# The key compares of the count table: four slots in one fp16 tensor-tensor compare, read by PE with a step

## The chip, the cores and the metric

The kernel runs on one core of one Trainium2 chip. The metric is the device time of one execution in microseconds. The kernel before took 5724.34 us, the median of three runs (5718.58 to 5726.55). Engines are called by their names in the profile: PE (TensorE, with PEld for its weight loads), DVE (VectorE), ACT (ScalarE), POOL (GpSimd), SP (SyncE, which here only issues DMAs; SPq is its queue).

## The reference, cut to what matters

Four graph layers run one after the other on 6250 nodes of 128 features and 100000 edges `(src, dst)`, sorted by `dst`. The first of them is, three times:

```python
msgs = h[src] * (src != dst)
agg = segment_sum(msgs, dst, num_segments=N)
x_neigh = agg @ W_conv[l] + b_conv[l]
h = relu(concatenate([x_neigh, h]) @ W_upd[l] + b_upd[l])
```

The sum over edges is linear in `h`, so it is a product with a table of counts: how many edges go from node `src` to node `dst`. The kernel builds this table once and uses it in three layers here and again in the last graph layer. Only the building of the table is touched by the change.

## The kernel before, in words

**The table.** It is the DRAM tensor `A_d`, 128 partitions (the low seven bits of `src`) by strips of `KEYS` = 392 fp16 numbers (49 blocks of `src` times 8 neighbouring `dst`). It is built in `BSLOTS` = 1184 slots. A slot takes 256 edges as two halves (`h` or `k` 0 and 1) of 128 edges, one edge per partition. For each half DVE writes two one-hot matrices: `src_hot`, which of 128 source rows the edge has, and `key_hot`, which of the 392 keys it has. PE multiplies them, 128 weight columns (`src_hot`) by 392 moving columns (`key_hot`), and adds into a PSUM bank.

**The DVE part** (lines 915 to 931). A group is `HOTS` = 4 slots, so there are 296 groups. At the head of a group, one tensor-tensor compare (line 924) writes the `src_hot` of all four slots and both halves: 128 rows by 8 = 1024 fp16 elements, in which the 8 values of a row lie side by side. It compares `count_up` (each number repeated eight times) with `vals` (the eight values of the group, repeated over the rows). Then each slot has two tensor-scalar compares (line 928), one for each half, of the contiguous row of 392 keys with one number per partition. `key_hot` has a buffer for each of four slots; the slot's buffers are free when PE has counted the slot four earlier (line 926). `hots_ready` goes up by one for each slot.

**The PE part** (lines 1588 to 1600). For each slot PE waits until ACT has emptied far enough (`evacuated`, line 1593), clears a bank with a matmul of one column and zero weights (line 1594), waits for `src_ready` and `hots_ready`, and issues the two matmuls of line 1598, which raise `counted`. The weights are read from `src_hot` with a step of 8 elements (16 bytes); the moving matrix `key_hot` is contiguous. Every four slots PE loads eight bank numbers into registers (line 429, called at 1591).

**The ACT and SP part.** ACT copies one bank per slot from PSUM into one of eight fp16 strips in SBUF (lines 1287 to 1294), once `counted` has it and the DMA that last read this strip has landed (`strip_out`). SP writes the strip to `A_d` with one DMA per slot (line 501), 98 KB, and loads eight row numbers into registers every eight slots (line 429, called at 499). The order on each queue is the program's order; no queue has other work in this stage. POOL waits for a DMA of this stage and does nothing in it.

**After the stage**, SP waits until all strips are in DRAM (lines 502 to 507) and loads the first blocks of the table (line 516); DVE removes the self loops from them (line 941) and PE multiplies (line 1634), which is the layer loop.

**Buffers.** `rg` holds `key_hot` and the two buffers of `src_hot`; `count_up` and `src_val` lie in plane 1 of `planes`, which is read again as table blocks after the stage.

Of the kernel before, what the change touches and what calls it, by code (L numbers as in the profile page):

```python
# [28 lines left out]
P = 128  # L29
# [31 lines left out]
KEYS = BLOCKS * STRIP  # L61
# [5 lines left out]
BSLOTS = -(-(ES_TILES + STRIPS + 1) // BODY) * BODY  # L67
BJ = -(-BSLOTS // P)
BPAD = BJ * P
BK = -(-ES_TILES // P)  # L70
BANKS = 8
# [3 lines left out]
HOTS = 4  # L75
# [57 lines left out]
def gnn(nc, io, out):  # L133
    fp32, i32, bf16, fp16 = mybir.dt.float32, mybir.dt.int32, mybir.dt.bfloat16, mybir.dt.float16
    DVE = mybir.EngineType.DVE
    ALU, ACT = mybir.AluOpType, mybir.ActivationFunctionType

    ctx = ExitStack()
    with ctx:
# [22 lines left out]
        pl = sb("planes", [P, 6, NP_])  # L162
# [3 lines left out]
        rg = sb("rg", [P, 2624])  # L166
# [42 lines left out]
        flat = ps[:, :, :].rearrange("p b n -> p (b n)")  # L209
# [22 lines left out]
        hots_ready, counted, evacuated = sem("hots_ready"), sem("counted"), sem("evacuated")  # L232
        src_ready = sem("src_ready")
# [117 lines left out]
        colT = pl[:, 0, 0:4 * BPAD].rearrange("p (w h s) -> p w h s", w=2, h=2)  # L351
        steps = pl[0:1, 5, 0:4 * BPAD].bitcast(i32)
        oh = onehot[:, :, :, :].rearrange("p a g n -> p (a g n)")
        key_row = oh[:, 0:KEYS // 2].bitcast(fp16)
# [5 lines left out]
        plan_i = oh[:, 624:624 + 4 * BJ].bitcast(i32).rearrange("p (j c) -> p j c", c=4)  # L360
        tiles_f = oh[:, 672:672 + 3 * BK].rearrange("p (n k) -> p n k", k=BK)
        tiles_i = oh[:, 688:688 + 2 * BK].bitcast(i32).rearrange("p (n k) -> p n k", k=BK)
        key_hot = rg[:, 0:HOTS * KEYS].bitcast(fp16).rearrange("p (b h n) -> p b h n", b=HOTS, h=2)
        src_hot = rg[:, HOTS * KEYS:HOTS * (KEYS + 2 * P)].bitcast(fp16).rearrange("p (b n t) -> p b n t", b=2, t=2 * HOTS)
        count_up = pl[:, 1, 2600:2600 + HOTS * P].bitcast(fp16).rearrange("p (n t) -> p n t", t=2 * HOTS)
        src_val = pl[:, 1, 3200:3200 + BPAD].bitcast(fp16).rearrange("p (h s) -> p h s", h=2)
        strips = scaled[:, :, :].rearrange("p a n -> p (a n)")[:, 0:BODY * KEYS // 2].bitcast(fp16).rearrange("p (b n) -> p b n", b=BODY)


# [76 lines left out]
        def _(sp):  # L446
# [49 lines left out]
            for s in range(BSLOTS):  # L496
                b = s % BODY
# [5 lines left out]
                sp.wait_ge(strip_out[b], 16 * (BSLOTS // BODY + 1))  # L503
            sp.wait_ge(st_plan, 64)

            sp.wait_ge(hots_ready, BSLOTS)
            sp.wait_ge(src_ready, BSLOTS // HOTS)
            for n in range(LAYERS * VB):
                u = n % VB
                k = VB_COLS[u] // STRIP  # L510
# [35 lines left out]
            for q in range(PAIRS):  # L546
# [7 lines left out]
                for u in (2 * q, 2 * q + 1):  # L554
                    k = VB_COLS[u] // STRIP
# [93 lines left out]
        def _(dve):  # L649
# [89 lines left out]
            for k in range(SJ):  # L739
                last = dve.tensor_scalar(cmp[:, k, :], iota_s, small[:, 2, k:k + 1], None, ALU.is_ge)  # L740
# [68 lines left out]
            def step(ins):  # L809

                planned_so_far[0] += 1
                ins.then_inc(planned, 1)
                dve.wait_ge(planned, planned_so_far[0])
# [12 lines left out]
            for k in range(BK):  # L826
                last = dve.tensor_scalar(later[:, k, 0:lead], at_slot, tiles_f[:, 1, k:k + 1], None, ALU.is_gt)
# [85 lines left out]
                    dve.tensor_tensor(q_rows[0][:, cut, 2, :], by_block(hb_rest[:, (c - 1) % 2, :]), q_rows[0][:, cut, 1, :], ALU.subtract).then_inc(q_low, 1)  # L913

            for h in range(2):
                last = dve.tensor_copy(src_val[:, h, :], colT[:, 1, h, :])
            step(last)
            step(dve.tensor_copy(count_up, key_row[:, 0:P].rearrange("p (n o) -> p n o", o=1).broadcast_to([P, P, 2 * HOTS])))
            for s in range(BSLOTS):
                if s % HOTS == 0:  # L920

                    dve.wait_ge(counted, BANKS + max(s - HOTS, 0))
                    vals = src_val[:, :, s:s + HOTS].rearrange("p (o h) s -> p o h s", o=1).broadcast_to([P, P, 2, HOTS])
                    dve.tensor_tensor(src_hot[:, s // HOTS % 2].rearrange("p n (h s) -> p n h s", h=2), count_up.rearrange("p n (h s) -> p n h s", h=2),
                                      vals, ALU.is_equal).then_inc(src_ready, 1)
                dve.wait_ge(counted, BANKS + s + 1 - HOTS)
                for h in range(2):
                    last = dve.tensor_scalar(key_hot[:, s % HOTS, h, :], key_row, colT[:, 0, h, s:s + 1], None, ALU.is_equal)  # L928
                last.then_inc(hots_ready, 1)

            dve.wait_ge(counted, BANKS + BSLOTS)

# [36 lines left out]
            for l in range(LAYERS):  # L969
                for u in range(VB + 2):  # L970
                    n, w = l * VB + u, VB_COLS[min(u, VB - 1)]
# [98 lines left out]
            for c in range(CHUNKS + LAG_O):  # L1070
# [5 lines left out]
                k = c - LAG_O  # L1076
# [15 lines left out]
            for c in NORM_V:  # L1092
                for b in range(c * CB, (c + 1) * CB):
                    last = dve.tensor_scalar(rows_view(3)[:, b, :], rows_view(1)[:, b, :], stat[:, 4, b:b + 1], stat[:, 1, b:b + 1], ALU.mult, ALU.add)
# [104 lines left out]
            for q in range(PAIRS + 1):  # L1199
                for k in range(TWOS if q < PAIRS else AT_SPLIT[1] + 1):  # L1200
                    if q < PAIRS:
# [8 lines left out]
                        n = IN_TWO[k]  # L1210
# [255 lines left out]
        def _(pe):  # L1466
# [121 lines left out]
            for s in range(BSLOTS):  # L1588
                b = s % (BODY // 2)
                if b == 0:  # L1590
                    banks = steps_at(mybir.EngineType.PE, 2 * s, BODY, (BANKS - 1) * 512)

                pe.wait_ge(evacuated, s + BANKS - 5)
                pe.matmul(flat[:, bass.ds(banks[2 * b], 1)], no_weights, key_row[:, 0:1], start=True, stop=True, skip_group_check=True)  # L1594
                pe.wait_ge(src_ready, s // HOTS + 1)
                pe.wait_ge(hots_ready, s + 1)
                for k in range(2):
                    last = pe.matmul(flat[:, bass.ds(banks[2 * b + 1], KEYS)], src_hot[:, s // HOTS % 2, :, k * HOTS + s % HOTS], key_hot[:, s % HOTS, k, :],  # L1598
                                     start=False, stop=True, skip_group_check=True)
                last.then_inc(counted, 1)  # L1600

# [321 lines left out]
```

## Time and profile before

| what | value |
|---|---|
| median of three runs | 5724.34 us |
| the profiled execution, from its first to its last instruction (span) | 5771.7 us |
| PE busy / DVE busy / ACT busy, share of the span | 86% / 63% / 47% |
| the stage of the count table, first to last strip DMA issued | 109.6 to 866.7 us |
| DVE / PE / ACT busy in 400 to 600 us, in the midst of it | 97% / 81% / 73% |

The profile gives for the profiled execution its span alone; no time around the span is shown for it. "Busy" is the time in which an engine ran an instruction that counts; the issue of a DMA does not count, so SP has no busy share. A group row reads: line, engine, operation, output<-input, count | busy us, mean ns of one | idle us before, and what ended that idle time. Durations of instructions that follow each other closely overlap in their pipelines, so the start-to-start time can be shorter than the duration.

### The profile page before, as it was taken

To read this page: it belongs to the slowest core of one execution; us is meant where nothing else is said; L and a number is where in the kernel's file an instruction comes from. 1 tells how busy PE (TensorE), PEld (TensorE's weight loads), DVE (VectorE), ACT (ScalarE), POOL (GpSimd) and SP (SyncE) were. 2 spreads that over 40 slices of the span, in tenths; PEclk is the share of its full clock that TensorE was granted. 3 is DMA by queue.
4 is the path that set the end of the run, shared out by engine and by line. 5 is a ranking of instruction groups with operands and counts; after the bars stand their busy time and mean duration, and the time that the engine had idled before them with its cause. 6 is when DMAs were issued, how large, how long until landed. Compare 5 with 4: busy or idle time off the path is not lost.

```text
span 5771.7 us, 104492 instructions
## 1 busy us (share of the span) xinstructions
PE 4992.4 (86%) x27719; PEld 3586.0 (62%) x27720; DVE 3660.0 (63%) x9507; ACT 2739.6 (47%) x7037; POOL 1847.7 (32%) x1948
## 2 busy tenths in 40 slices
PE   5888879999999997888888888688888888899998
PEld 3444447888888885444444444566666566677775
DVE  7999994443433444666666667555555555588886
ACT  4777771111111114766677667322222222488884
POOL 0000001100000002666666665566666666111111
PEclk9999999999999998888889888799999999999999
DMA  4554556555555552111112111233333333233330
GB/s 97 161 159 157 160 160 220 197 188 179 191 185 199 194 187 72 45 45 45 45 45 46 44 45 43 79 88 86 86 88 86 87 87 86 78 115 137 137 125 28
DMA packets 388581, 650.09 MB, mean 113 GB/s; under 512 B 91140, under 2 KB 329694, under 8 KB 363179
## 3 DMA queue, kind: packets, MB, share of 16 engines
q1 hardware_dynamic: 330844, 526.22, 27.4%
q0 software_dynamic: 57424, 120.01, 8.4%
q8 instruction: 157, 2.57, 0.2%
q14 instruction: 156, 1.28, 0.1%
HBM read 511.57 MB, written 134.42 MB: 112 GB/s over the span
## 4 chain that ended last, share of the span: by engine, by line
PE 55%; another core or an unknown queue 13%; DVE 9%; issue 9%; ACT 6%; SPq 3%; DMA 3%; DVEq 2%; POOL 1%; ACTq 0%; POOLq 0%
PE ps L1634 21%; PE ps L1691 14%; PE ps L1829 8%; SPq L501 3%; PE ps L1598 2%; DMA A_d<-scaled 2%; PE ps L1690 2%; PE ps L1519 2%; ACT ps L1401 1%; ACT scaled L1294 1%; DVE rg L928 1%; ACT planes L1406 1%; DVE planes L1047 1%; DVE onehot L795 1%
## 5 line engine op out<-in xcount | busy, mean ns | idle before, releaser
L575 POOL DMA_INDIRECT rg<-tab_L,idxT x832 | 811.8, 976 | 1499.5 <-DMA tab_L<-planes 1025.9
L1634 PE MATMUL ps<-planes 128*128 128x384 bf16 (+1 forms) x7350 | 1224.6, 327 | 20.0 <-DVE planes L941 16.6
L1634 PEld LDWEIGHTS ps<-planes 128*128 128x128 f16 (+1 forms) x7350 | 1036.8, 142 | 172.2 <-issue 22.3
L1354 ACT ACTIVATE scaled<-onehot,rg 128x128 f32<-128x128 f32 x2912 | 893.2, 388 | 397.9 <-PE ps L1691 230.8
L1691 PE MATMUL ps<-scaled,rg 128*128 128x512 f32 x1664 | 1032.2, 714 | 0.0
L1690 PEld LDWEIGHTS ps<-rg,onehot 128*128 128x128 f32 x1664 | 342.7, 215 | 747.9 <-issue 401.7
L1294 ACT ACTIVATE scaled<-ps 128x392 f16 x1184 | 547.9, 499 | 209.9 <-DMA A_d<-scaled 133.4
L805 DVE TENSOR_TENSOR planes<-planes,ps 128x128 f32 x832 | 239.5, 288 | 570.0 <-remote 473.2
L928 DVE TENSOR_SCALAR rg<-onehot,planes 128x392 f16<-128x392 f16 x2368 | 580.1, 320 | 16.5 <-PE ps L1598 11.7
L1598 PE MATMUL ps<-rg 128*128 128x392 f16 x2368 | 562.6, 362 | 25.4 <-DVE rg L928 5.0
L1047 DVE TENSOR_TENSOR planes<-planes,ps 128x512 f32 x832 | 571.8, 687 | 16.0 <-issue 13.0
L1396 ACT ACTIVATE planes<-ps,cols 128x512 f32<-128x512 f32 x208 | 143.0, 687 | 912.8 <-remote 883.3
L1437 ACT ACTIVATE scaled<-ps,att 128x256 f32<-128x256 f32 x1225 | 504.1, 499 | 113.3 <-DVE dlLT L1211 38.6
L1313 ACT ACTIVATE rg<-rg 128x128 bf16<-128x128 f32 (+1 forms) x150 | 46.4, 309 | 1059.6 <-DVE rg L992 1059.6
L621 POOL DMA_INDIRECT rg<-tab_L,idxT x416 | 398.6, 958 | 281.7 <-remote 145.2
L621 POOL DMA_INDIRECT planes<-tab_L,idxT x416 | 393.4, 946 | 244.1 <-remote 146.0
L1690 PE MATMUL ps<-rg,onehot 128*128 128x5 f32 x1664 | 272.0, 234 | 221.8 <-ACT scaled L1354 64.7
L988 DVE COPY rg<-ps 128x128 f32<-128x128 f32 (+1 forms) x150 | 44.2, 295 | 574.2 <-PE ps L1634 574.2
L1045 DVE TENSOR_TENSOR planes<-planes,ps 128x5 f32 x832 | 133.9, 161 | 388.5 <-PE ps L1691 223.1
L1598 PEld LDWEIGHTS ps<-rg 128*128 128x128 f16 x2368 | 246.0, 155 | 139.7 <-issue 38.7
L1594 PE MATMUL ps<-onehot 128*128 128x1 f16 x1184 | 202.4, 171 | 112.7 <-ACT scaled L1294 83.8
L1145 DVE TENSOR_TENSOR_SCAN planes<-planes,ps 128x512 f32<-128x512 bf16 x208 | 266.1, 1279 | 52.3 <-ACT ps L1401 31.6
(282 smaller groups left out, 7790.5 us busy)
## 6 DMA issues: line engine op xcount, KB each, us to landing
planes<-A_d SPq DMA_DIRECT2D x196, 1568.0 KB, 8.4
A_d<-scaled SPq DMA_DIRECT2D x1184, 98.0 KB, 1.7
planes<-rows_d SPq DMA_DIRECT2D x209, 256.0 KB
rg<-tab_L,idxT POOLq DMA_INDIRECT x1248
planes<-tab_L,idxT POOLq DMA_INDIRECT x416
real_row<-real_d SPq DMA_DIRECT2D x200, 32.0 KB, 5.0
planes<-w_d SPq DMA_DIRECT2D x209, 9.0 KB
tab_L<-planes SPq DMA_DIRECT2D x7, 476.0 KB, 3.1
```

Of the source, the lines that this page charges most:

```text
L575: pool.indirect_dma_start(ring[:, q * GROUP + g, 0:width], None, table[:, :], bass.IndirectOffsetOnAxis(idxT[:, at:at + 1], 0)).then_inc(g ...
L621: pool.indirect_dma_start(max_rows[q * GROUP + g], None, tab2[:, :], bass.IndirectOffsetOnAxis(idxT[:, at:at + 1], 0)).then_inc(max_rows_i ...
L928: last = dve.tensor_scalar(key_hot[:, s % HOTS, h, :], key_row, colT[:, 0, h, s:s + 1], None, ALU.is_equal)
L1047: dve.tensor_tensor(at, at, ps[:, 2 * (s % 4), :].rearrange("p (m n) -> p m n", n=P), ALU.add).then_inc(acc_done, 1)
L1294: act.activation(strips[:, b, :], flat[:, bass.ds(banks[b], KEYS)], ACT.Copy).then_inc(evacuated, 1)
L1354: last = act.activation(scaled[:, s % 4, m * P:(m + 1) * P], onehot[:, q % 2, g, :], ACT.Copy, scale=ring[:, s, D + m:D + m + 1])
L1437: last = act.activation(gate[:, t % 4, :, :, j], ps_adv(q).rearrange("p (i n) -> p i n", i=2), ACT.Sigmoid, bias=att[:, 2 * k + j, 0:1])
L1598: last = pe.matmul(flat[:, bass.ds(banks[2 * b + 1], KEYS)], src_hot[:, s // HOTS % 2, :, k * HOTS + s % HOTS], key_hot[:, s % HOTS, k, :] ...
L1634: last = pe.matmul(ps_agg(u), a_blk[n % ABUF][:, 0:w, k], q_rows[l % 2][:, k].rearrange("p t n -> p (t n)"), start=(k == 0), stop=(k == BL ...
L1690: pe.matmul(ps[:, 2 * (s % 4) + 1, 0:MIX + 1], onehot[:, q % 2, g, :], ring[:, s, D:D + MIX + 1], start=True, stop=True)
L1691: pe.matmul(ps[:, 2 * (s % 4), :], ring[:, s, 0:D], scaled[:, s % 4, :], start=True, stop=True).then_inc(mm_done, 1)
L1829: last = pe.matmul(ps_pair(q), rows_view(3)[:, 2 * k + j, :], weight[t % 3][:, :, :, j].rearrange("p i n -> p (i n)"), start=(k == 0 and j ...
```

## The change

One buffer of `key_hot` now holds the one-hots of a whole group of four slots, both halves: 392 keys by 8 fp16 elements, the 8 values of one key side by side, as `src_hot` already has them. One tensor-tensor compare per group writes it, in place of eight tensor-scalar compares. There are two such buffers, one in `rg` and one in plane 1. PE reads the 392 moving columns of a slot and half with a step of 8 elements (16 bytes) instead of contiguously. `count_up` grows from 128 to 392 numbers repeated eight times, and the key values are cast to fp16 into `key_val` as the source values were. `hots_ready` counts groups, and PE waits for the group's. DVE waits once per group, for the group two earlier to be counted. SP has one more wait ahead of its first load of table blocks.

```diff
-        key_hot = rg[:, 0:HOTS * KEYS].bitcast(fp16).rearrange("p (b h n) -> p b h n", b=HOTS, h=2)
+        KH = HOTS * KEYS
+        key_hot = [t.bitcast(fp16).rearrange("p (n t) -> p n t", t=2 * HOTS) for t in (rg[:, 0:KH], pl[:, 1, KH:2 * KH])]
...
-        count_up = pl[:, 1, 2600:2600 + HOTS * P].bitcast(fp16).rearrange("p (n t) -> p n t", t=2 * HOTS)
-        src_val = pl[:, 1, 3200:3200 + BPAD].bitcast(fp16).rearrange("p (h s) -> p h s", h=2)
+        count_up = pl[:, 1, 0:KH].bitcast(fp16).rearrange("p (n t) -> p n t", t=2 * HOTS)
+        key_val, src_val = (pl[:, 1, 2 * KH + n * BPAD:2 * KH + (n + 1) * BPAD].bitcast(fp16).rearrange("p (h s) -> p h s", h=2) for n in range(2))
...
-            sp.wait_ge(hots_ready, BSLOTS)
+            sp.wait_ge(hots_ready, BSLOTS // HOTS)
+            sp.wait_ge(counted, BANKS + BSLOTS)
...
             for h in range(2):
+                dve.tensor_copy(key_val[:, h, :], colT[:, 0, h, :])
                 last = dve.tensor_copy(src_val[:, h, :], colT[:, 1, h, :])
             step(last)
-            step(dve.tensor_copy(count_up, key_row[:, 0:P].rearrange("p (n o) -> p n o", o=1).broadcast_to([P, P, 2 * HOTS])))
-            for s in range(BSLOTS):
-                if s % HOTS == 0:
-
-                    dve.wait_ge(counted, BANKS + max(s - HOTS, 0))
-                    vals = src_val[:, :, s:s + HOTS].rearrange("p (o h) s -> p o h s", o=1).broadcast_to([P, P, 2, HOTS])
-                    dve.tensor_tensor(src_hot[:, s // HOTS % 2].rearrange("p n (h s) -> p n h s", h=2), count_up.rearrange("p n (h s) -> p n h s", h=2),
-                                      vals, ALU.is_equal).then_inc(src_ready, 1)
-                dve.wait_ge(counted, BANKS + s + 1 - HOTS)
-                for h in range(2):
-                    last = dve.tensor_scalar(key_hot[:, s % HOTS, h, :], key_row, colT[:, 0, h, s:s + 1], None, ALU.is_equal)
-                last.then_inc(hots_ready, 1)
+            step(dve.tensor_copy(count_up, key_row.rearrange("p (n o) -> p n o", o=1).broadcast_to([P, KEYS, 2 * HOTS])))
+
+            def hots(to, values, s, n):
+
+                vals = values[:, :, s:s + HOTS].rearrange("p (o h) s -> p o h s", o=1).broadcast_to([P, n, 2, HOTS])
+                return dve.tensor_tensor(to.rearrange("p n (h s) -> p n h s", h=2), count_up[:, 0:n].rearrange("p n (h s) -> p n h s", h=2),
+                                         vals, ALU.is_equal)
+
+            for s in range(0, BSLOTS, HOTS):
+                dve.wait_ge(counted, BANKS + max(s - HOTS, 0))
+                hots(src_hot[:, s // HOTS % 2], src_val, s, P).then_inc(src_ready, 1)
+                hots(key_hot[s // HOTS % 2], key_val, s, KEYS).then_inc(hots_ready, 1)
...
-                pe.wait_ge(hots_ready, s + 1)
+                pe.wait_ge(hots_ready, s // HOTS + 1)
                 for k in range(2):
-                    last = pe.matmul(flat[:, bass.ds(banks[2 * b + 1], KEYS)], src_hot[:, s // HOTS % 2, :, k * HOTS + s % HOTS], key_hot[:, s % HOTS, k, :],
+                    last = pe.matmul(flat[:, bass.ds(banks[2 * b + 1], KEYS)], src_hot[:, s // HOTS % 2, :, k * HOTS + s % HOTS], key_hot[s // HOTS % 2][:, :, k * HOTS + s % HOTS],
                                      start=False, stop=True, skip_group_check=True)
```

## Rows read from the trace of the kernel before

**Rows 1.** The page's first line.

```profile
span 5771.7 us, 104492 instructions
```

**Rows 2.** Groups by line, 100 to 880 us: busy, mean | idle before, releasers.

```profile
L928 DVE TENSOR_SCALAR rg<-onehot,planes 128x392 f16<-128x392 f16 x2368 | 580.1, 320 | 16.5 <-PE ps L1598 11.7
L1598 PE MATMUL ps<-rg 128*128 128x392 f16 x2368 | 562.6, 362 | 25.4 <-DVE rg L928 5.0 <-issue 1.1
L1294 ACT ACTIVATE scaled<-ps 128x392 f16 x1184 | 547.9, 499 | 209.9 <-DMA A_d<-scaled 133.4 <-PE ps L1598 55.4 <-issue 5.2
...
L924 DVE TENSOR_TENSOR rg<-planes 128x1024 f16<-128x1024 f16 x296 | 203.8, 688 | 0.0
```

**Rows 3.** Line 501, SP's strip DMAs: duration min/median/max, first and last start.

```profile
L501 SPq DMA_DIRECT2D A_d<-scaled x1184: 332/332/2113, 109.6 to 866.7; - x198
```

**Rows 4.** Waits of SP's queue, 110 to 865 us: total, times, longest.

```profile
SPq L501 <- ACT scaled L1294: 6.0, 11, 3.1
```

**Rows 5.** The chain of waits, 440 to 470 us: start, us, what.

```profile
440.90 1.84 SPq L501
...
452.46 0.33 SPq L501
...
452.98 0.33 SPq L501
...
454.38 0.53 SPq L429
```

**Rows 6.** Waits of all engines, 105 to 870 us: total, times, longest.

```profile
ACT scaled L1294 <- DMA A_d<-scaled: 133.4, 169, 2.6
PE ps L1594 <- ACT scaled L1294: 83.8, 186, 2.1
```

**Rows 7.** DVE in order of time, 440 to 470 us: start, us, engine, line.

```profile
450.73 0.68 DVE L924 TENSOR_TENSOR rg<-planes 128x1024 f16<-128x1024 f16 x1
451.34 1.94 DVE L928 TENSOR_SCALAR rg<-onehot,planes 128x392 f16<-128x392 f16 x8
453.19 0.68 DVE L924 TENSOR_TENSOR rg<-planes 128x1024 f16<-128x1024 f16 x1
```

**Rows 8.** In order of time, the start of the stage.

```profile
107.90 1.55 DVE L916 CAST planes<-planes 128x1280 f16<-128x1280 f32 x2
...
109.49 0.69 DVE L918 COPY planes<-onehot 128x1024 f16<-128x1024 f16 x1
...
111.62 0.87 PE L1598 MATMUL ps<-rg 128*128 128x392 f16 x2 [4.57 <-DVE rg L928]
```

**Rows 9.** PE in order of time, 440 to 460 us.

```profile
442.43 0.17 PE L1594 MATMUL ps<-onehot 128*128 128x1 f16 x1
442.46 0.53 PE L1598 MATMUL ps<-rg 128*128 128x392 f16 x2
442.82 0.17 PE L1594 MATMUL ps<-onehot 128*128 128x1 f16 x1
```

**Rows 10.** Groups of DVE by form, whole span.

```profile
L1047 DVE TENSOR_TENSOR planes<-planes,ps 128x512 f32 x832 | 571.8, 687 | 16.0 <-issue 13.0 <-PE ps L1691 1.6 <-remote 1.2
...
L941 DVE SCALAR_TENSOR_TENSOR planes<-real_row,slot_id,planes 128x128 f16<-128x128 bf16 x291 | 206.8, 912 | 39.1 <-DMA planes<-A_d 39.0
...
L996 DVE TENSOR_TENSOR rg<-rg 128x128 f32<-128x128 f32 x147 | 43.0, 293 | 55.2 <-ACT rg L1313 55.2
```

**Rows 11.** Groups of PE's weight loads by form, whole span.

```profile
L1634 PEld LDWEIGHTS ps<-planes 128*128 128x128 f16 x7203 | 1013.0, 142 | 171.9 <-issue 22.3 <-DVE planes L956 3.8
...
L1598 PEld LDWEIGHTS ps<-rg 128*128 128x128 f16 x2368 | 246.0, 155 | 139.7 <-issue 38.7
...
L1594 PEld LDWEIGHTS ps<-onehot 128*128 128x128 f16 x1184 | 117.8, 100 | 252.2 <-issue 224.4
```

**Rows 12.** Line 1829 in order of time: four matmuls, moving step 8 bytes.

```profile
5201.05 1.07 PE L1829 MATMUL ps<-dlT,planes 128*128 128x256 f32 x4
```

**Rows 13.** Line 1691, moving contiguous fp32: duration min/median/max, first and last start.

```profile
L1691 PE MATMUL ps<-scaled,rg x1664: 592/676/1202, 2275.0 to 3562.6; 128*128 128x512 f32 x185
```

## The prediction

> **What bounds the kernel now.** I read the busy shares first, then the stage's groups, then who waits for whom, then each queue in order of time. The span is 5771.7 us [rows 1]. The change touches one stage of it, the count table, in which SP issues its 1184 strip DMAs from 109.6 to 866.7 us [rows 3], that is 757.1 us. What lies before and after is the same program.
>
> By busy time the stage belongs to DVE: 580.1 us in the key compares and 203.8 in the source compares, with 16.5 us of idle [rows 2]. A group of four slots takes DVE from one source compare to the next 453.19 - 450.73 = 2.46 us, of which 0.61 is the source compare and 1.85 the eight key compares [rows 7]. 296 groups by 2.455 are 727 us, so DVE alone would need 30 us less than the stage takes.
>
> The queue without a busy share is the tighter one. SP waited for ACT 6.0 us in all, 3.1 of them in one wait [rows 4]. Otherwise its issues follow each other at 452.98 - 452.46 = 0.52 us, and every eight of them it loads registers for 0.53 us [rows 5]: 8 x 0.517 + 0.55 = 4.69 us for eight slots, 148 x 4.69 = 694 us. The rest of the 757, about 60 us, are 6 of waiting and some long issues, such as the one of 1.84 us [rows 5], with a median of 0.332 and a longest of 2.113 [rows 3]. So in the profiled execution SP is the bound, DVE is 4% behind, and that SP is the slow one is seen upstream: ACT stands 133.4 us waiting for a strip's DMA and PE 83.8 us for ACT [rows 6].
>
> PE has room. When nothing holds it, a slot takes 442.82 - 442.43 = 0.39 us: 0.03 for the clearing matmul and 0.36 for the two of 392 columns [rows 9]. Two times 392 columns in 0.36 us is 2.2 columns per ns, so the clock is at its 2.4 GHz level, where 392 columns are 163 ns. Four slots are 1.58 us of the group's 2.46. These 0.88 us are what the change can use up.
>
> **The change part by part.**
>
> DVE, removed: eight tensor-scalar compares per group, 1.85 us start to start [rows 7]. Added: one tensor-tensor compare of 392 x 8 = 3136 fp16 elements. fp32 tensor-tensor takes 687 ns for 512 elements and 293 for 128 [rows 10]: 1.03 ns per element and 162 ns fixed. The source compare takes 688 ns for 1024 fp16 elements of just the form to be added [rows 2]: (688 - 162) / 1024 = 0.514 ns per element, two at a time. So 162 + 3136 x 0.514 = 1774 ns, and 0.08 less start to start (the source compare: 0.688 against 0.61 [rows 7]), 1.70 us. The bounds are narrow, since form and types are those of the source compare: 1.65 to 1.80. A group becomes 0.61 + 1.70 = 2.31 us, 0.15 less; over 296 groups DVE gains 43 us. While SP bounds the stage none of it counts.
>
> Set-up: two more casts of 1280 elements (the two take 1.55 us), `count_up` with 3136 in place of 1024 elements, 162 + 1613 = 1.78 in place of 0.69 us [rows 8], and PE's first matmuls wait for a whole key compare, 1.70 us, in place of two compares of 0.23 each. That is 1.55 + 1.09 + 1.24 = 3.9 us. PE's first matmul of line 1598 moves from 111.6 [rows 8] to 115.5 us. No cover: SP's second DMA waits for just this.
>
> Waits: DVE now waits once per group for the group two earlier; behind it on DVE there is only this stage. With two buffers the group's period is the longest of DVE's 2.31, PE's time, and half of both with the hand-overs, (2.31 + PE + some 0.5) / 2. PE can no longer start on the first slot of a group while the others are written, which costs only the start counted above. SP's added wait on `counted` comes when the last strip has landed, long after the last matmul: nothing. Registers that PE loads every four slots are loaded while matmuls that were already released run; if not, they add up to 0.3 us per group to a PE that is the bound.
>
> PE's moving operand: a step of 16 bytes at one column per 0.417 ns. No row shows this for a moving operand. The nearest rows are the weight loads of the same one-hots. Line 1598 loads 128 columns at a step of 16 bytes in 155 ns, line 1634 at 98 bytes in 142 and line 1594 contiguous columns in 100 [rows 11]. The step costs 55 ns for 128 columns, 0.43 ns per column, which is about one more cycle at 2.4 GHz for each. Applied to 392 columns that is 168 ns, and the matmul doubles from 163 to 331 ns. From the 98-byte row it is 0.33 ns per column, 292 ns. The lower bound is no cost: at a step of 8 bytes line 1829's four fp32 matmuls of 256 columns take 1.07 us [rows 12], at most 1.05 ns per column, where the shortest contiguous fp32 matmul of line 1691 takes 592 ns for 512, 1.16 per column [rows 13]. No halving there, but it is half of this step, and an fp32 column takes over twice the time of an fp16 one. The far upper row is DVE's line 941, which reads and writes 128 elements 98 bytes apart in 912 ns, where contiguous ones take 293 [rows 10]: 4.8 ns per element, and the stage would take over twice as long. I take 331 ns: same data, same step, same engine.
>
> The Trainium skill speaks of this step: Advanced Engine Details and Errata, SBUF Cachelines, says that lines are 16 bytes long and that at least two accesses must hit a line to absorb its latency. Here each column would be on a line of its own, which it says is penalised without giving a price; the rise from 100 to 155 ns in the weight loads [rows 11] agrees in sign. The Trainium skill's SBUF — State Buffer, section Door 1: The DMA port swizzle, counts 8 bf16 elements as a stride that is still free. By that sentence the step costs nothing and the result is the first rival's. The two give no common answer for exactly 16 bytes.
>
> Sum of the forecast. The shorter first: with long matmuls the exposed 37 ns between a slot's two (0.36 less 2 x 163) are covered, and a slot takes 0.03 + 2 x 0.331 = 0.69 us; if nothing is covered it takes 0.39 + 2 x 0.168 = 0.73. I take 0.705, 2.82 us per group. That is above DVE's 2.31, SP's 2.35 (2.56 with the long issues), and (2.31 + 2.82 + 0.5) / 2 = 2.8. 296 x 2.82 = 835 us; PE ends at 115.5 + 835 = 950 instead of 862 us: +88 us in the profiled execution.
>
> The profiled span is 47 us above the median of the runs. If this lies in part in SP's long issues, the stage of the runs shown is shorter now, down to DVE's 727, while the PE-bound stage after the change is not shortened by it: +88 to +118. I take +96: 5724 + 96 = 5820 us.
>
> **The rivals.**
>
> A, the step is free, or costs less than the room. Up to 0.60 us per slot (matmuls of 285 ns, 1.75 times today's) PE stays below SP's 0.64. Then SP bounds the stage as before, DVE's 43 us are hidden behind it, and the late start remains: +4, 5728 us. If SP's long issues belong to the profiled execution alone, DVE's 727 are the stage today and SP's 700 tomorrow: -27 + 4 at most, of which I give half; 5700 to 5728, centre 5719. For it: the 8-byte row [rows 12] and that the weight loads' 55 ns might be lost on fetching pairs of weights, which a moving operand does not do. Against: 155 over 100 ns at this step [rows 11].
>
> B, the other side: faster. One mechanism: in the runs shown DVE is the bound, 98% busy, and a free step lets its 0.15 us per group through until SP's 4.69 per eight slots stops it. It decides from 11 us net on, and needs SP's long issues below some 30 of their 60 us. Place: lines 924 and 928; price: -15 to -23 us, 5705 us.
>
> C, more than double: strided columns at 2 ns or more each, as DVE's row hints. 2 x 0.8 + 0.03 = 1.6 us per slot, +1150 us, 6900.
>
> D, the step halves the rate only partly, 1.75 to 1.85 times: the stage grows by 0 to 45 us, 5728 to 5770.
>
> **How the numbers follow.** The forecast (doubled columns) 0.56; A without B 0.22; B 0.14; C 0.02; D 0.06. Within 0.2% (11 us, about what a measurement of this kernel can tell from no change) fall A and a little of D: 0.23. Faster is B, 0.14. Slower is the rest, 0.63. The likeliest case has its own range: 0.69 us per slot with a stage of 757 now gives +70 (5794), 0.73 with 727 now gives +141 less what SP and the registers share, 5850. Leaving out most of B and C, the range is 5710 to 5850.
>
> **What would show it.** DVE: key compares x296 of about 1775 ns. PE: line 1598's start-to-start of 0.33 us and a mean duration near 530 against 362 now [rows 2]; the stage's last matmul near 950 us; DVE waiting for PE some 0.5 us in every group; SP waiting for ACT, and ACT for PE, where both stood on DMAs. The first matmul at 115.5. Wrong: matmuls still 363 ns long and the last strip issued near 870; then A or B holds, and SP's waits decide between them. A key compare at 1 element per 1.04 ns (3.4 us, 4.0 us per group) would make DVE the bound and break the DVE step.

## The result

The changed kernel takes 6650.33 us (median of four runs, 6646.04 to 6654.92) against 5724.48 us for the kernel before (now the median of four runs): 1.162 times the kernel before, 95% interval 1.160 to 1.164, 926 us more. The forecast was slower, 5820 us, with a range of 5710 to 5850. The sign was right and the size was wrong by a factor of almost ten (926 us against 96).

### The profile after

From the page: the span, the busy tenths of four engines in 40 slices of the span, and PE's granted clock in tenths of full speed.

```profile
span 6644.2 us, 102423 instructions
...
PE   5999999999999999999788888886888888899998
PEld 3222222222388888888444444445666666677775
DVE  6444444444344344343666666675555555568886
ACT  3333333333211111112677776773222222268885
...
PEclk8555555555599999999899898987999999999999
```

The count table now fills about ten slices of 166 us, in all of which PE is busy and its clock is granted at half, the 1.2 GHz level. Line 501 is line 502 now, its strip DMAs: duration, then first and last start, where [rows 3] had 109.6 to 866.7.

```profile
L502 SPq DMA_DIRECT2D A_d<-scaled x1184: 332/332/871, 111.4 to 1790.2; - x198
```

The stage takes 1678.8 us against 757.1, 921.7 more. With its start 1.8 us later that is 923.5 of the 926. The two spans differ by 872.5 us only, since after the last strip DMA the profile of the kernel before runs on for 4905.0 us and this one for 4854.0, in code that the change does not touch. The profile of `contig` below has 4902.4 us there, on a chip on which the kernel before takes 5767.8 us; so the 51 us fit a difference between chips. The stage does not differ like this: the contiguous rows of `pairs` need 758.7 us for it on one chip, and those of `weights` 758.5 on another.

The groups of the stage (100 to 1820 us), which answer to [rows 2]; line 1598 is 1601 now, 924 and 928 are 926, 1294 is 1297. Both buffers stand apart, and the x444 are the 296 source compares and the 148 key compares into `rg`, so their mean mixes two shapes:

```profile
L1601 PE MATMUL ps<-planes,rg 128*128 128x392 f16 x1184 | 856.5, 863 | 0.0
L1601 PE MATMUL ps<-rg 128*128 128x392 f16 x1184 | 856.1, 862 | 8.4 <-DVE rg L926 8.4
L1297 ACT ACTIVATE scaled<-ps 128x392 f16 x1184 | 588.4, 497 | 1092.9 <-PE ps L1601 1090.8 <-DVE planes L915 2.1
L926 DVE TENSOR_TENSOR rg<-planes 128x1024 f16<-128x1024 f16 (+1 forms) x444 | 456.7, 1056 | 958.9 <-PE ps L1601 958.9
L926 DVE TENSOR_TENSOR planes<-planes 128x3136 f16<-128x3136 f16 x148 | 264.1, 1784 | 0.0
```

The matmul's mean went from 362 to 863 ns, ACT and DVE wait for PE, 1091 and 959 us, and in the stage none of the three waits for a DMA. In order of time, one slot and DVE beside it (start, us, engine, line, and in brackets the idle time before it):

```profile
603.44 0.18 PE L1597 MATMUL ps<-onehot 128*128 128x1 f16 x1
...
603.49 1.55 PE L1601 MATMUL ps<-rg 128*128 128x392 f16 x2
603.66 0.69 DVE L926 TENSOR_TENSOR rg<-planes 128x1024 f16<-128x1024 f16 x1 [3.26 <-PE ps L1601]
...
604.27 1.78 DVE L926 TENSOR_TENSOR planes<-planes 128x3136 f16<-128x3136 f16 x1
...
604.85 0.19 PE L1597 MATMUL ps<-onehot 128*128 128x1 f16 x1
```

A slot is 604.85 - 603.44 = 1.41 us against 0.39 unhindered in [rows 9]. From the starts of all 2368 matmuls, the second of a slot holds PE for a median of 689 ns, 1.76 ns per column. That is 2.1 cycles at the granted clock or 4.2 at the full one, so the trace alone leaves two causes open: two cycles per column at a clock that stands at half, or a fixed time per column, whatever the clock. DVE is as predicted, a compare of 1784 ns, and has 3.26 us of idle in each group. The clock did not fall in the stage. In both kernels it is at half already when PE's first matmul of the stage comes, after 4.57 us of idle in [rows 8] and 8.37 us here. Only the kernel before then goes to full: 0.99 in 125 to 200 us, against 0.50 here to the end.

### The profile page after: what moved, and what is told of

Its sections match the earlier page's. It is cut to its first block, busy times and chain, and to the rows that moved or that the text cites. A ratio compares the mean times of both kernels' runs of the same rounds, so it can differ in the third digit from the quotient of the medians.

```text
span 6644.2 us, 102423 instructions
## 1 busy us (share of the span) xinstructions
PE 6026.6 (91%) x27719; PEld 3595.3 (54%) x27720; DVE 3634.3 (55%) x7437; ACT 2777.3 (42%) x7037; POOL 1848.9 (28%) x1948
## 4 chain that ended last, share of the span: by engine, by line
PE 68%; another core or an unknown queue 14%; DVE 6%; issue 5%; ACT 5%; DVEq 1%; POOL 0%; ACTq 0%; DMA 0%; POOLq 0%; SPq 0%
PE ps L1601 25%; PE ps L1637 18%; PE ps L1694 10%; PE ps L1832 7%; ACT ps L1404 2%; PE ps L1693 2%; ACT planes L1409 2%; PE ps L1522 1%; DVE planes L1050 1%; PE ps L1504 1%; PE ps L1648 1%; PE ps L1645 0%; ACT planes L1266 0%; DVE scaled L1035 0%
## 5 line engine op out<-in xcount | busy, mean ns | idle before, releaser
L1297 ACT ACTIVATE scaled<-ps 128x392 f16 x1184 | 588.4, 497 | 1092.9 <-PE ps L1601 1090.8
L1694 PE MATMUL ps<-scaled,rg 128*128 128x512 f32 x1664 | 1011.1, 700 | 0.0
L926 DVE TENSOR_TENSOR rg<-planes 128x1024 f16<-128x1024 f16 (+1 forms) x444 | 456.7, 1056 | 958.9 <-PE ps L1601 958.9
L1601 PE MATMUL ps<-rg 128*128 128x392 f16 x1184 | 856.1, 862 | 8.4 <-DVE rg L926 8.4
L1601 PE MATMUL ps<-planes,rg 128*128 128x392 f16 x1184 | 856.5, 863 | 0.0
L1597 PEld LDWEIGHTS ps<-onehot 128*128 128x128 f16 x1184 | 148.6, 125 | 609.2 <-issue 609.2
```

Of the source, the lines that this page charges most:

```text
L926: return dve.tensor_tensor(to.rearrange("p n (h s) -> p n h s", h=2), count_up[:, 0:n].rearrange("p n (h s) -> p n h s", h=2), vals, ALU.i ...
L1297: act.activation(strips[:, b, :], flat[:, bass.ds(banks[b], KEYS)], ACT.Copy).then_inc(evacuated, 1)
L1694: pe.matmul(ps[:, 2 * (s % 4), :], ring[:, s, 0:D], scaled[:, s % 4, :], start=True, stop=True).then_inc(mm_done, 1)
```

## The experiments

The experiments were run on two chips, and each ratio is against the kernel before on the same chip. The chips differ: the kernel before takes 5767.8 us on the first (`sweep`, `mix`, `contig`, `pairs`) and 5276.1 on the second (the others). `sweep`, `mix`, `contig` and `weights` are for timing: PE reads other elements of the same buffers, so the table's contents are not the right ones. `sweep`, `mix` and `weights` ran once each. In the cuts of code `...` stands for what is left out. Theories: R, two array cycles for each column on a 16-byte line of its own; M, a fixed time of the memory side per line; G, a cost that grows with the step, as more lines are touched.

**sweep: eight steps in one kernel**

```diff
+                step = 1 + s // 148
                 for k in range(2):
...
+                    row = key_hot[s // HOTS % 2].rearrange("p n t -> p (n t)")[:, 0:step * KEYS].rearrange("p (n t) -> p n t", t=step)[:, :, 0]
...
```

> Timing only: the kernel after, but PE's 392 moving columns start at the buffer's first element and have a step of 1 in the first 148 slots, 2 in the next 148, and so on to 8 in the last 148 (contents of the count table are wrong). Theory R (a column costs more once each lies on a 16-byte line of its own, and the clock at half is a second effect): matmuls of 163 ns start to start for steps 1 to 7 and a jump at 8 alone, to some 680 ns with the clock granted at 0.5. Theory G (cost grows with the step, as more lines are touched per column): a slope from step 2 or 4 on, e.g. 1 / 1 / 1 / 1 / 1.25 / 1.5 / 1.75 / 2 times. Theory L (any step over 1 breaks the fast read): doubled from step 2 on. If a stretch with a cost already falls to the clock of 0.5, it reads 2 x 327 ns and not 327.

The matmul reads `row`. Line 1603, its matmuls of one buffer within the stretches of steps 1, 2, 3, 4, 5, 6, 7 and 8: duration min/median/max, then first and last start.

```profile
L1603 PE MATMUL ps<-planes,rg x120: 329/363/534, 129.7 to 198.8; 128*128 128x392 f16 x120
L1603 PE MATMUL ps<-rg x112: 332/375/542, 220.8 to 288.3; 128*128 128x392 f16 x112
L1603 PE MATMUL ps<-planes,rg x127: 423/448/481, 310.4 to 389.9; 128*128 128x392 f16 x127
L1603 PE MATMUL ps<-planes,rg x128: 508/526/540, 410.1 to 500.0; 128*128 128x392 f16 x128
L1603 PE MATMUL ps<-rg x125: 592/596/611, 520.5 to 629.8; 128*128 128x392 f16 x125
L1603 PE MATMUL ps<-planes,rg x132: 682/692/701, 649.4 to 788.0; 128*128 128x392 f16 x132
L1603 PE MATMUL ps<-rg x131: 768/772/786, 809.6 to 969.8; 128*128 128x392 f16 x131
L1603 PE MATMUL ps<-rg x128: 852/861/869, 999.3 to 1179.5; 128*128 128x392 f16 x128
```

From step 3 to 8 the median duration grows by 83 ns per element of step. The time for which the slot's second matmul holds PE, start to start (medians over 148 slots), and the mean clock granted in the stretch:

| step, elements | 1 | 2 | 3 | 4 | 5 | 6 | 7 | 8 |
|---|---|---|---|---|---|---|---|---|
| ns | 166 | 173 | 261 | 347 | 432 | 519 | 605 | 689 |
| clock | 0.96 | 0.95 | 1.00 | 1.00 | 0.52 | 0.50 | 0.50 | 0.50 |

From step 3 on this is proportional to the step: 347 / 4 = 86.8, 689 / 8 = 86.1 ns. 392 columns at step s touch 392 x s / 8 lines of 16 bytes, so one line takes 689 / 392 = 1.76 ns. At steps 1 and 2 the 49 and 98 lines (86 and 172 ns) are about covered by the 163 ns of the columns. R is refuted, since it wanted no cost below step 8 and has step 8 at about the right value only by chance (2 x 327 ns at half clock). So is the third theory of the expectation, a doubling from step 2 on. G is right in kind, with a slope, and far off in size: 4.2 times at step 8, not 2. The clock was at 1.00 through steps 3 and 4 and fell to half at 510 us, when step 5 had begun and PE was busy without a pause. The whole run took 6100.4 us.

**mix: other pairs of steps, and half as many columns**

```diff
+                steps, n = ((1, 8, KEYS), (8, 8, KEYS), (1, 1, KEYS), (4, 8, KEYS), (1, 1, KEYS), (8, 8, KEYS // 2), (16, 16, KEYS // 2), (1, 16, KEYS // 2))[s // 148][0:2], \
+                    KEYS if s // 148 < 5 else KEYS // 2
...
+                    row = key_hot[s // HOTS % 2].rearrange("p n t -> p (n t)")[:, 0:steps[k] * n].rearrange("p (n t) -> p n t", t=steps[k])[:, :, 0]
...
```

> Timing only: the kernel after with other steps per stretch of 148 slots, for the slot's two matmuls: (1,8), (8,8), (1,1), (4,8), (1,1), and then with 196 columns (8,8), (16,16), (1,16); contents wrong. Question: is the 1.73 ns per column of the kernel after a fixed time of the memory side, or two array cycles at whatever clock is granted? Theory R (two cycles): in (1,8), if the clock is granted at 1.0 there, the stepped matmul takes 2 x 163 = 327 ns; at 0.5 it takes 654. Theory M (fixed time of about 1.7 ns per column): 676 ns at either clock. The half clock in (8,8) returns to 1.0 in (1,1) if it is the stalled columns that lower it. Step 16 with 196 columns: the same time as step 8 (98 columns' worth doubled, 327 to 340 ns at half clock) if the line of its own is all that counts, longer if distance counts.

A pair such as (1,8) gives the steps of a slot's two matmuls. Line 1604 with 196 columns, at step 8 and then at step 16. Behind it three windows, in the stretches (1,1), (8,8) with 196 and (16,16) with 196 columns: start and end, length, the busy us (and count) of PE, PEld, DVE, ACT and POOL, then the granted clock, the DMA share and GB/s.

```profile
L1604 PE MATMUL ps<-planes,rg x134: 508/520/529, 829.6 to 924.6; 128*128 128x196 f16 x134
...
L1604 PE MATMUL ps<-planes,rg x130: 512/526/537, 939.7 to 1034.7; 128*128 128x196 f16 x130
```

```profile
485.00:565.00 80.00, 64.71 (x384) 39.53 (x384) 75.05 (x66) 57.70 (x127) 0.00 (x0) 0.96 0.49 156
...
825.00:925.00 100.00, 99.83 (x411) 45.77 (x410) 81.41 (x68) 68.25 (x139) 0.00 (x0) 0.50 0.46 145
940.00:1035.00 95.00, 95.00 (x386) 43.21 (x385) 76.95 (x65) 63.87 (x129) 0.00 (x0) 0.50 0.43 138
```

Step 8 with 196 columns touches 196 lines at a clock of 0.50 and holds PE for 347 ns; step 4 with 392 columns touches 196 lines too, at a clock of 1.00 in the sweep, and takes 347. The number of lines sets the time and the clock does nothing to it: M. Step 16 takes 354 ns with as many lines, so distance beyond a line costs almost nothing, which G's growth with the step would not give. The cost follows the step up to 8 elements and then grows by 2% to step 16, so the unit that counts is 16 bytes, within 2%. The stepped matmul of 392 columns takes 692 ns in (1,8) and 691 in (4,8), as beside another stepped one. In both stretches the clock was at 0.50, so the test I had planned there, a stepped matmul of 392 columns at full clock, did not come about; the two with 196 lines stand in for it. The clock was at 0.96 and 0.98 in the two stretches of (1,1) and went back to 0.50 in the stretches behind them: it follows the stepped reads and is no cause here. The run took 6035.6 us.

**contig: the change without its step**

```diff
-                    last = pe.matmul(... key_hot[s // HOTS % 2][:, :, k * HOTS + s % HOTS],
+                    row = key_hot[s // HOTS % 2].rearrange("p n t -> p (n t)")[:, (k * HOTS + s % HOTS) * KEYS:(k * HOTS + s % HOTS + 1) * KEYS]
+                    last = pe.matmul(... row,
```

> Timing only: the kernel after, except that PE reads 392 contiguous elements of the same key buffers (so it counts wrong keys). This leaves the compare, the set-up, the waits per group and the buffers of the change, and takes away the step alone. If the step is the whole loss (my reading of the trace after): within 0.5% of the kernel before, 5695 to 5735 us; rival A of the prediction says +4, rival B says -15 to -23 us. If the coarser hand-over of groups or the contention of a 3136-element compare with PE has a part in the 926 us, it stays well above 5750.

Measured 5771.07 against 5767.83 us, 1.0007 (0.9997 to 1.0017): with the step taken away and all else kept, no loss is left. The waits of SP's queue from 125 to 862 us (total, times, longest; the kernel before has 1.9, 5, 0.4 there), and the window from 120 to 862 us, with DVE busy 684 of 742 us and PE 601:

```profile
SPq L502 <- ACT scaled L1297: 1.5, 4, 0.4
```

```profile
120.00:862.00 742.00, 600.56 (x3544) 365.47 (x3542) 684.07 (x588) 541.95 (x1182) 0.00 (x0) 0.96 0.51 161
```

DVE has 58 us of room in this window and the stage is as long as before, since SP still waits for next to nothing once the stage runs, as in [rows 4]. At the start SP's second strip DMA follows the first after 7.45 us instead of 3.63: the 3.8 us of the later first matmul.

**pairs: contiguous rows from one compare per group**

```diff
+        key_hot = [t.rearrange("p n t -> p (n t)").rearrange("p (t n) -> p t n", t=2 * HOTS) for t in key_hot]
...
-                dve.tensor_copy(key_val[:, h, :], colT[:, 0, h, :])
+                dve.tensor_copy(key_val.rearrange("p (g h s) q -> p h g s q", h=2, s=HOTS)[:, h],
+                                colT[:, 0, h, :].rearrange("p (g s o) -> p g s o", s=HOTS, o=1).broadcast_to([P, BPAD // HOTS, HOTS, 2]))
...
+                return dve.tensor_tensor(key_hot[s // HOTS % 2].rearrange("p t (m q) -> p t m q", q=2),
+                                         key_row.rearrange("p (o m q) -> p o m q", o=1, q=2).broadcast_to([P, t, KEYS // 2, 2]),
+                                         key_val[:, 2 * s:2 * s + t, :].rearrange("p t (o q) -> p t o q", o=1).broadcast_to([P, t, KEYS // 2, 2]), ALU.is_equal)
...
-                    last = pe.matmul(... key_hot[s // HOTS % 2][:, :, k * HOTS + s % HOTS],
+                    last = pe.matmul(... key_hot[s // HOTS % 2][:, k * HOTS + s % HOTS, :],
```

> A complete version: each key value is stored twice, side by side, so that one tensor-tensor compare writes eight contiguous rows of 392 keys (innermost two elements, both inputs with step 1), and PE reads contiguously. If DVE keeps two elements per cycle in this form, a compare is 1.78 us as in the kernel after and the time is that of the kernel with contiguous reads, 5695 to 5735 us. If the form with only two innermost elements falls to one per cycle, a compare is 3.4 us, the group 4.0 us, and the time about 5724 + 296 x 1.5 = 6180 us.

Measured 5771.55 against 5767.83 us, 1.0006 (0.9996 to 1.0015). The compare keeps its rate with only two innermost elements, 1785 ns against 1784 in the kernel after. One of its two groups on DVE, and the source compare's:

```profile
L936 DVE TENSOR_TENSOR rg<-onehot,planes 128x3136 f16<-128x3136 f16 x148 | 264.2, 1785 | 0.0
...
L930 DVE TENSOR_TENSOR rg<-planes 128x1024 f16<-128x1024 f16 x296 | 203.4, 687 | 59.0 <-PE ps L1612 58.2
```

DVE is idle for 59 us now, where [rows 2] had 16.5: what it gained it waits. The kernel is no faster, since SP bounds it as it did before.

**split_before: a quarter of the strip DMAs on POOL's queue**

```diff
...                                   # SP's loop over the slots
+                if b % 4 == 3:
+                    continue
...
+            for s in range(BSLOTS):
...                                   # POOL's: b, and eight row numbers loaded every eight slots
+                if b % 4 == 3:
+                    pool.wait_ge(evacuated, BANKS + s + 1)
+                    pool.dma_start(A_d[:, bass.ds(rows[b], 1), :], strips[:, b:b + 1, :]).then_inc(strip_out[b], 16)
```

> The kernel before, with the strip DMAs of slots 3 and 7 of every eight issued from POOL's queue, which is idle in this stage; all else as before. It tests which engine bounds the stage. Theory SP: SP's queue is the bound (6 issues of 0.52 and one register load of 0.6 us leave 3.7 us for eight slots, against 4.7); the stage falls to DVE's 727 us plus a few, -20 to -28 us, 0.35 to 0.5% faster. Theory DVE: SP only follows DVE; no change within 0.1%. Rival: POOL's DMAs land late and hold ACT, or POOL takes the port that DVE's tensor-scalar compares use; slower.

Measured 5259.1 against 5276.08 us, 0.9965 (0.995 to 0.998), 17 us faster, a little less than the 20 to 28 expected. SP's strip DMAs, and DVE's key compares:

```profile
L503 SPq DMA_DIRECT2D A_d<-scaled x888: 332/332/1956, 109.9 to 844.1; - x178
```

```profile
L938 DVE TENSOR_SCALAR rg<-onehot,planes 128x392 f16<-128x392 f16 x2368 | 578.6, 330 | 4.1 <-PE ps L1608 3.1
```

SP ends 23 us earlier than in [rows 3], DVE has 4.1 us of idle instead of 16.5, and takes 330 instead of 320 ns for a compare, 24 us over the 2368 of them. So DVE bounds the stage now, at 734 us.

**split_pairs: the same for the version with contiguous rows**

> The complete version with contiguous rows from one compare per group, and the strip DMAs of slots 3 and 7 of every eight on POOL's queue. Theory SP: with SP off the path, DVE's 2.31 us per group bound the stage, 684 us plus the later start of 3.9: -60 us or so, 1.0% faster than the kernel before, and some 40 us faster than the kernel before with split DMAs. Rival: ACT (0.46 us per slot, register loads on top) or the hand-over of whole groups takes over near 0.6 us per slot, and the gain stays under 30 us.

Measured 5220.42 against 5276.08 us, 0.9895 (0.988 to 0.991), 56 us faster, and the fastest of all the versions; some 60 were expected. SP's strip DMAs and DVE's source compares:

```profile
L507 SPq DMA_DIRECT2D A_d<-scaled x888: 332/332/2166, 111.2 to 803.7; - x178
```

```profile
L940 DVE TENSOR_TENSOR rg<-planes 128x1024 f16<-128x1024 f16 x296 | 202.9, 686 | 2.2 <-PE ps L1622 1.5
```

SP's last strip DMA starts 63 us earlier than in [rows 3], with DVE at 2.2 us of idle. So two bounds lay close together: SP first, DVE 4% behind, as the prediction had them, and the faster compare pays only once SP is relieved.

**four: the change with half the step**

```diff
+        key_hot = [t.rearrange("p n t -> p (n t)").rearrange("p (h n s) -> p h n s", h=2, s=HOTS) for t in key_hot]
...
-                    last = pe.matmul(... key_hot[s // HOTS % 2][:, :, k * HOTS + s % HOTS],
+                    last = pe.matmul(... key_hot[s // HOTS % 2][:, k, :, s % HOTS],
```

The buffer is [partition, half, key, slot] here, and the key compare of DVE writes it in this order, still once per group.

> A complete version of the change with a step of half the size: four values of a key side by side (one half of four slots), so the step is 4 elements, 8 bytes. Theory line (a moving operand reads one 16-byte line per 1.75 ns, whatever the clock; two columns per line here): matmuls of 346 ns, a slot 0.725 us, the stage 117 to 975 us against 862, +105 to +110 us, 1.9% slower, with the clock near 1.0. If only a line of its own per column costs, as in the prediction: no change.

Measured 5392.08 against 5276.08 us, 1.022 (1.020 to 1.023), +116 us, some 6 more than by the line theory. Half of line 1608's matmuls, and the window of 400 to 800 us, with the clock behind POOL's 0.00 (x0):

```profile
L1608 PE MATMUL ps<-rg x1184: 508/526/548, 116.2 to 976.8; 128*128 128x392 f16 x198
```

```profile
400.00:800.00 400.00, 400.00 (x1647) 179.36 (x1646) 328.19 (x276) 272.16 (x549) 0.00 (x0) 1.00 0.44 139
```

The clock stayed at 1.00 and the loss is there. At half the step a slot takes 0.729 us start to start, so the four of a group take 2.92 us, more than the 2.46 of [rows 7].

**weights: the weight loads at steps 1 to 8, moving rows contiguous**

```diff
-                    last = pe.matmul(... src_hot[:, s // HOTS % 2, :, k * HOTS + s % HOTS], ...
+                    last = pe.matmul(... src_hot[:, s // HOTS % 2].rearrange("p n t -> p (n t)")[:, 0:P * (1 + s // 148)].rearrange("p (n t) -> p n t", t=1 + s // 148)[:, :, 0], key_hot[s // HOTS % 2][:, k * HOTS + s % HOTS, :],
```

All else is as in `pairs`.

> Timing only: the complete version with contiguous moving rows, but the 128 weight columns start at the first element and have a step of 1 in the first 148 slots, 2 in the next, up to 8 in the last (contents wrong). It asks why the prediction's weight-load row misled. Theory four streams (a load reads four streams of 32 columns at once, each one line per 1.75 ns): duration constant near 100 ns while a stream's lines are hidden, then growing by 32 x 1.75 / 8 = 7 ns per step, 155 at step 8 and 127 at step 4. Theory prediction (the step costs 0.43 ns for each of 128 columns and only beyond one column per line): 100 ns up to step 7 and 155 at step 8.

Line 1612's weight loads at steps 1, 4, 7 and 8: duration min/median/max.

```profile
L1612 PEld LDWEIGHTS ps<-planes,rg x132: 95/96/152, 120.0 to 198.3; 128*128 128x128 f16 x132
L1612 PEld LDWEIGHTS ps<-planes,rg x136: 111/114/151, 400.3 to 483.1; 128*128 128x128 f16 x136
L1612 PEld LDWEIGHTS ps<-planes,rg x140: 130/145/157, 681.0 to 769.5; 128*128 128x128 f16 x140
L1612 PEld LDWEIGHTS ps<-planes,rg x130: 141/160/171, 780.2 to 859.3; 128*128 128x128 f16 x130
```

For steps 1 to 8 the medians of the slots' first loads are 96, 97, 103, 112, 117, 125, 132 and 143 ns, and those of their second loads 96, 98, 104, 118, 128, 143, 154 and 167. From step 3 on that is a slope of 8.0 and of 12.6 ns per step. Four streams of 32 columns would give 32 x 1.76 / 8 = 7.0, two streams of 64 would give 14, one of 128 would give 28, and the prediction's reading gave nothing before step 8. The 127 ns that the four-stream theory expected at step 4 were 112 and 118. The rise with every step is shown, and so is that it is far below one stream's. That there are four streams fits the first loads and not the second, which these runs do not explain; no run counts them. The run took 5276.6 us against 5276.1: the slower loads cost nothing here.

## Why the prediction was wrong in size

- **The bound of the stage**: right. SP is the bound and DVE just behind it, by `contig`, `pairs`, `split_before` and `split_pairs`. That PE bounds it after the change was right too: PE is idle for 8.5 us in it, 8.4 of them before its first matmul of line 1601.
- **DVE's compare**, 1774 ns: measured 1784. The 43 us it frees are hidden, as said.
- **Set-up**, PE's first matmul at 115.5: measured 117.24, of which 1.8 are a later start of the whole stage.
- **Waits per group, buffers, SP's added wait**: costed at nothing, and `contig` finds +0.07%, with zero in its interval (-0.03 to +0.17%).
- **The moving operand's step: this is the step that failed.** It took 155 - 100 = 55 ns from the weight-load rows [rows 11] and divided by 128 columns, 0.43 ns per column, and added this to the 0.417 ns of a contiguous column: 331 ns a matmul, 2.82 us a group. Measured were 676 ns for a slot's first matmul and 689 for its second, and 1.413 us a slot, 5.65 a group. The step's price is 1.76 ns for each 16-byte line, and it is not added to the column's time: the larger of the two counts (`sweep`, `mix`). The difference of 1.413 and 0.705 us over 1184 slots is 838 us; with the 88 that the prediction had for its slot of 0.705 us in the profiled execution these are the 926. Why the weight-load row misled is in part inferred. If a load reads four streams of 32 columns at once, its 55 ns are the price of 32 lines, 1.72 ns each, and 392 of those are 674 ns; then the right row was used with the wrong divisor. The Trainium skill says of this, in TensorE: Matmul & The Clock Gate, section Weight-path perf modes, that the weight is split into four parallel chunks. In `weights` the first loads agree with it (8.0 ns per step against 7.0), and the second do not (12.6).
- **The second row that would have told**: line 1829's 256 columns 8 bytes apart [rows 12] touch 128 lines, by the law 128 x 1.76 = 225 ns; four such matmuls in 1.07 us leave 0.23 between starts once the last one's duration of 0.39 is taken off, and the median over the whole trace is 0.227. I read it as free, because an fp32 column takes long enough to hide nearly all of it: from start to start a contiguous matmul of 512 fp32 columns (line 1691) takes 429 ns at the least, 0.84 per column, so 256 take some 215. My 1.05 and 1.16 ns per column came from durations with their tails, and by starts the step of 8 bytes costs 12 ns, not less than nothing.
- **The clock**: I assumed the 2.4 GHz level. It stood at the 1.2 GHz level for the whole stage, but `mix` against `sweep` shows that this cost the stepped matmuls nothing (347 ns at either).
- **The rival that came closest** is C, 2 ns or more per column (1.76 measured), at a chance of 0.02 and priced at +1150 us. DVE's row [rows 10] had been its only support. The range ended at the doubled rate, although the bounds went on to 4.8 ns per column; a cost that no row showed, on an engine with 0.88 us of room in 2.46, deserved a range up to there.
- **The median against the span**: I took the 47 us between them for a cost of the profiled execution. The changed kernel's profiled execution is 2 us from its device time (6646.04 against a span of 6644.2), and the kernel before takes 5767.8 us on the first chip of the experiments, where the part behind the stage is as long as in the profile of the kernel before (4902.4 us in `contig`, 4905.0). So the difference is more likely one of chips, and the 8 us that I added for it had no ground.
- **The two sentences on cachelines** (the Trainium skill's Advanced Engine Details and Errata, SBUF Cachelines, and the Trainium skill's SBUF — State Buffer, Door 1: The DMA port swizzle): the trace agrees in sign with the first, that a line must serve at least two accesses, but two are not enough for fp16 moving columns: two per line (step 4) cost 347 ns against 166. The second, that 8 bf16 elements are a free stride, fails here for PE's moving operand of fp16, with 689 ns.

## What to carry to other kernels

In these runs a matmul whose fp16 moving operand has a step held PE for the larger of its columns' time and 1.76 ns for each 16-byte line, so the step was nearly free up to 2 elements (173 ns against 166) and made the matmul 4.2 times as long at 8. Lay the one-hots out so that the compare writes contiguous rows: repeating each value twice, side by side, was enough for DVE to keep its rate (`pairs`). When a price is read off another instruction, as here a weight load's, look for a second row with the step in question on the operand in question, and let the range reach the far row when there is none. Before an engine is made faster, look at the queue that has no busy share: SP waited for 6 of this stage's 757 us and was in no view of busy engines.

## What the runs showed that I had not expected

- The price of a line does not depend on the granted clock: 196 lines took 347 ns at 1.00 (392 columns, step 4) and at 0.50 (196 columns, step 8).
- PE can be 100% busy in the profile with the clock at half for 1665 us (125 to 1790): the clock stayed at 1.00 with two fp16 columns per line (step 4, 392 columns) and was at half from step 5 on, and with 196 columns at step 8.
- In `split_before` both of DVE's compares were longer, the tensor-scalar one 330 ns against 320 and the source compare 698 against 688, and POOL took a median of 968 ns to issue a strip DMA. In `split_pairs` the source compare took 686 ns, the key compare 1784, and POOL 539. This looks as if POOL's issues and the tensor-scalar compares get in each other's way; no run tests it, and the 320 and 688 are from another chip.
